# The feed-forward's second product: one 512-column matmul for both parts of the weights, and two VectorE sums for the halves

## The chip, the cores and the metric

The kernel runs on one core of a Trainium2 chip. The time is the device time of one execution in microseconds. The kernel before took 990.59 us (median of 3 runs, 989.98 to 991.91). The profiled execution took 988.45 us, of which its trace spans 986.7 us.

## The reference

It is one decoder block on 4 sequences of 1024 tokens with width 256: causal self-attention, cross-attention to 154 context tokens, both with 16 heads, and a feed-forward of width 1024, each added to the running `x`.

```python
nx = _ln(x, ln1_scale, ln1_bias);  qkv = nx @ W_qkv
x = x + _attend(q, k, v, causal) @ W_self_out
nx = _ln(x, ln2_scale, ln2_bias);  q, kv = nx @ W_q, encoder_output @ W_kv
x = x + _attend(q, k, v, None) @ W_cross_out
nx = _ln(x, ln3_scale, ln3_bias)
ffn = jax.nn.relu(nx @ W1 + b1) @ W2 + b2
return x + ffn
```

## The kernel before

One program of five instruction streams runs the stages in order: projections (A), self-attention, its output projection with the cross-attention's queries (C), cross-attention, and the last stage (E), which this change touches. Each engine works through its own stream in the order in which the code is written, and waits on semaphores. There is no scheduler.

Float32 products that need precision are made of three matmuls on rounded parts: each operand is split into a high part (its value rounded to the matmul's 32-bit format) and a low part (what is left). `product` (matmuls on lines 698, 699 and 700) adds high x low, low x high and high x high in the same accumulator. Every matmul loads its own stationary operand first.

Stage E treats 8 halves of a sequence (n = 0 to 7, 512 tokens each; `hf` is n's parity and picks its buffers). For one n:

- TensorE makes 8 feature blocks (`features_e`, f = 0 to 7, 512 tokens as columns, banks 0 and 1). Between them it makes the cross-attention's output projection for n + 1 (`project_e`).
- ScalarE applies bias and relu and rounds the result to `hT_hi`; VectorE makes `hT_lo` (line 1474). TensorE waits for each f by the semaphore `h_lo` in `part_in`.
- Then comes the second product, `relu(...) @ W2`, in four tiles t = 0 to 3 of 128 tokens and 256 output columns. The 8 feature blocks f are summed in a tile's accumulator. A bank holds 512 float32 columns, so tiles 0 and 1 fill bank 6 and tiles 2 and 3 fill bank 7. Once tile 1 is done TensorE transposes the normalised tokens of n + 1 (line 685, 8 transposes into banks 2 and 3), and goes on with tiles 2 and 3.
- ScalarE scales the transposed tokens of n + 1 (line 1023) and rounds them to `nT_hi` (line 1142); VectorE makes their low parts `nT_lo` (`scaled_low`, line 1429). Only behind this, in VectorE's stream, stand the two sums `xn = xt + bank` of n (line 1488, one for each bank, 512 columns), which free the banks by the semaphore `y_done`. `xt` holds the residual plus the bias `b2`.
- SyncE stores `xn` to the output after `y_done` (line 663).

`y_done` starts at 2, so that in n the tiles of bank 6 wait for the sum of bank 6 in n - 1, and the tiles of bank 7 for that of bank 7 in n - 1. The last n has no transposes and no `scaled_low`.

Of the kernel before, what the change touches and what calls it, by code (L numbers as in the profile page):

```python
# [5 lines left out]
ALU = mybir.AluOpType  # L6
# [4 lines left out]
F32R = mybir.dt.float32r  # L11

P = 128
# [5 lines left out]
def decoder_block_kernel(  # L19
# [3 lines left out]
    B, L, D = x.shape  # L23
# [4 lines left out]
    KC = D // P  # L28
    FC = F // P
    HF = 512  # L30
    TT = HF // P
# [32 lines left out]
    def tokens(ap, b, hf):  # L64
        return one(ap, b).rearrange("b (h t p) d -> p (b h) t d", p=P, t=TT)[:, hf]

    with ExitStack() as ctx:
        def sb(name, shape, dt=F32):
            return ctx.enter_context(nc.sbuf_tensor(name, shape, dt))

        def sem(name):
            return ctx.enter_context(nc.semaphore(name))

        bank = ctx.enter_context(nc.psum_tensor("bank", [P, 8, HF], F32))
# [31 lines left out]
        xt = sb("xt", [P, 2, TT, D])  # L106
# [6 lines left out]
        xn = sb("xn", [P, 2, TT, D])  # L113
# [38 lines left out]
        hT_hi, hT_lo = sb("hT_hi", [P, FC, HF], F32R), sb("hT_lo", [P, FC, HF], F32R)  # L152
        cT_hi, cT_lo = sb("cT_hi", [P, 2, KC, HF], F32R), sb("cT_lo", [P, 2, KC, HF], F32R)
        w1_hi, w1_lo = sb("w1_hi", [P, KC, F], F32R), sb("w1_lo", [P, KC, F], F32R)
        nT_hi, nT_lo = sb("nT_hi", [P, 2, KC, HF], F32R), sb("nT_lo", [P, 2, KC, HF], F32R)
        nxT_hi, nxT_lo = sb("nxT_hi", [P, 2, KC, HF], F32R), sb("nxT_lo", [P, 2, KC, HF], F32R)
        w2_hi, w2_lo = (t[:, :, :, :].rearrange("p h k (f d) -> p (h k f) d", d=D) for t in (nxT_hi, nxT_lo))
        wco_hi, wco_lo = sb("wco_hi", [P, KC, D], F32R), sb("wco_lo", [P, KC, D], F32R)
        HRING = 4
        hT = sb("hT", [P, HRING, HF])  # L160
# [46 lines left out]
        w_high, w_low = sem("w_high"), sem("w_low")  # L207
        wco_high, wco_low = sem("wco_high"), sem("wco_low")
        xb_ready = sem("xb_ready")
        f_ready, y_done = sem("f_ready"), sem("y_done")  # L210
        y_stored = [sem(f"y_stored{i}") for i in range(2)]

        class Attention:
# [168 lines left out]
        def _(sp):  # L382
            def load_x(ph, src, b, hf):
                sp.dma_start(xt[:, hf], tokens(src, b, hf)).then_inc(ph.x_in[hf], 16)
# [243 lines left out]
            def load_c(b, hf):  # L628
                if b == B - 1:
                    for half in range(2):  # L630
                        sp.wait_ge(XA.oC_stored[half], 16 + 16 * 2 * B)
                sp.dma_start(cT[:, hf], cross_ctx[bass.ds(2 * b, 2)].rearrange("c p t -> p c t")[:, :, HF * hf:HF * hf + HF]
                             ).then_inc(c_in[hf], 16)
# [20 lines left out]
            def store_e(b, left):  # L654
                for hf in range(2):
                    n = 2 * b + hf
                    if left > hf:
                        sp.wait_ge(E.xn_done, 2 + 2 * n + 4)
                        load_c(b + 1 + hf, 1 - hf)

                    for t0, t1 in ((0, TT),) if left or not hf else ((0, 2), (2, TT)):
                        sp.wait_ge(y_done, 2 + 2 * n + t1 // 2)
                        sp.dma_start(tokens(out, b, hf)[:, t0:t1],
                                     xn[:, hf, t0:t1]).then_inc(y_stored[hf], 16)
                    if left:
                        load_x(E, x1_dram, b + 1, hf)
# [3 lines left out]
            for b in range(B - 2):  # L670
                store_e(b, 2)
# [7 lines left out]
        def _(pe):  # L679
            def transposes(ph, n, hf, b0):  # L680

                pe.wait_ge(ph.nx_ready, n + 1)
                for k in range(KC):
                    for t in range(TT):
                        last = pe.transpose(bank[:, b0 + k, P * t:P * t + P], nx[:, hf, t, P * k:P * k + P], ident[:, :])  # L685
                    last.then_inc(ph.tp_ready, 1)
# [6 lines left out]
            def product(dst, terms, between=None):  # L693

                for j, (a_hi, a_lo, b_hi, b_lo) in enumerate(terms):
                    if between and j:
                        between(j - 1)
                    pe.matmul(dst, a_hi, b_lo, start=(j == 0), stop=False)  # L698
                    pe.matmul(dst, a_lo, b_hi, start=False, stop=False)  # L699
                    last = pe.matmul(dst, a_hi, b_hi, start=False, stop=(j == len(terms) - 1))  # L700
                return last
# [239 lines left out]
            def project_e(b, hf, i, o_bank=4):  # L941

                n = 2 * b + hf
                pe.wait_ge(c_lo, KC * n + KC)
                pe.wait_ge(E.xn_done, 2 + 2 * n + i - 1)
                for t in range(2 * i, 2 * i + 2):
                    last = product(bank[:, o_bank + i, D * (t % 2):D * (t % 2) + D],
                                   [(cT_hi[:, hf, k, P * t:P * t + P], cT_lo[:, hf, k, P * t:P * t + P], wco_hi[:, k, :],
                                     wco_lo[:, k, :]) for k in range(KC)])
                last.then_inc(E.o_ready, 1)  # L950
# [17 lines left out]
            def features_e(n, hf, f):  # L968
                pe.wait_ge(h_evac, 2 + FC * n + f - 1)
                product(bank[:, 1 - f % 2], [(w1_hi[:, k, P * f:P * f + P], w1_lo[:, k, P * f:P * f + P],  # L970
                                              nT_hi[:, hf, k, :], nT_lo[:, hf, k, :]) for k in range(KC)]
                        ).then_inc(h_ready, 1)
# [4 lines left out]
            def dense_e(b, more):  # L977
                for hf in range(2):
                    n = 2 * b + hf
                    ahead = hf == 0 or more  # L980
                    pe.wait_ge(nxT_low, 2 * n + 2)
                    for f in range(FC):
                        if n or f:
                            features_e(n, hf, f)
                        if f in PROJECT_AT and ahead:
                            pe.wait_ge(XA.acc_free, 2 + 2 * 4 * B)
                            project_e(b + hf, 1 - hf, PROJECT_AT.index(f))
                    pe.wait_ge(w_low, 3)


                    def part_in(f):
                        pe.wait_ge(h_lo, HRING + FC * n + f + 1)

                    for i in range(2):
                        pe.wait_ge(y_done, 2 + 2 * n + i - 1)
                        for t in range(2 * i, 2 * i + 2):
                            if t == 0:
                                part_in(0)
                            last = product(bank[:, 6 + i, D * (t % 2):D * (t % 2) + D],
                                           [(hT_hi[:, f, P * t:P * t + P], hT_lo[:, f, P * t:P * t + P], w2_hi[:, f, :], w2_lo[:, f, :])  # L1000
                                            for f in range(FC)], (lambda f: part_in(f + 1)) if t == 0 else None)
                        last.then_inc(f_ready, 1)
                        if i == 0 and ahead:
                            transposes(E, n + 1, 1 - hf, 2)

            pe.wait_ge(XA.exp_done, XA.SB + 4 * 4 * B * XA.NS)
# [161 lines left out]
        def _(dve):  # L1168
# [263 lines left out]
            def sums_e(b, hf, i, o_bank=4):  # L1432
                dve.wait_ge(y_stored[hf], 16 * b + 16)
                residual(E, b, hf, i, o_bank, 16)
# [33 lines left out]
            def dense_e(b, more):  # L1468
                for hf in range(2):
                    n = 2 * b + hf  # L1470
                    ahead = hf == 0 or more
                    for f in range(FC):
                        dve.wait_ge(h_hi, FC * n + f + 1)
                        dve.tensor_tensor(hT_lo[:, f, :], hT[:, f % HRING, :], hT_hi[:, f, :].bitcast(F32), ALU.subtract).then_inc(h_lo, 1)  # L1474
                        if f > PROJECT_AT[0] and f - PROJECT_AT[0] <= 2 and ahead:
                            sums_e(b + hf, 1 - hf, f - PROJECT_AT[0] - 1)
                        if f == PROJECT_AT[0] + 3 and ahead:
                            moments(E, xn, n + 1, 1 - hf)
                    if ahead:
                        normalize(E, xn, n + 1, 1 - hf)  # L1480
                    for k in range(KC) if more else ():
                        context_low(n + 2, hf, k)
                    if ahead:
                        scaled_low(n + 1, 1 - hf)
                    dve.wait_ge(xb_ready, n + 1)
                    for i in range(2):
                        dve.wait_ge(f_ready, 2 * n + i + 1)
                        dve.tensor_tensor(xn[:, hf, 2 * i:2 * i + 2, :], xt[:, hf, 2 * i:2 * i + 2, :],
                                          bank[:, 6 + i, :].rearrange("p (t d) -> p t d", t=2), ALU.add).then_inc(y_done, 1)

            dve.wait_ge(w_high, 2)
            dve.tensor_tensor(w2_lo, w2_sb[:, :, :], w2_hi.bitcast(F32), ALU.subtract).then_inc(w_low, 1)
# [219 lines left out]
```

## Time and profile before

| | |
|---|---|
| Median of 3 runs | 990.59 us |
| Profiled execution, and its span | 988.45 us, 986.7 us |
| TensorE busy with matmuls | 958.7 us (97%), 7632 matmuls |
| TensorE loading stationary operands | 599.0 us (61%) |
| VectorE busy | 742.7 us (75%) |
| ScalarE busy | 639.8 us (65%) |
| GpSimd busy | 257.2 us (26%) |
| Share of TensorE in the chain that ended last | 89% |

Busy time is a sum of the single instructions' durations where they don't overlap. A matmul's duration includes its way through the array, so two matmuls that follow each other overlap in the trace; what a matmul costs in a full stream is the distance between two starts, called its pitch here. "PEld" is the load of a stationary operand, which may run beside the matmul before it. A row of the timeline gives start, duration, engine, line, operation and count, and in brackets the idle time before it with what ended it.

### The profile page before, as it was taken

How to read it: one execution, taken by the hardware profiler on the slowest of the kernel's cores; microseconds unless marked ns; L12 is line 12 of the kernel's file. 1: busy time of each engine (PE TensorE's matmuls, PEld its weight loads, DVE VectorE, ACT ScalarE, POOL GpSimd, SP SyncE). 2: the span in 40 equal slices, each digit the busy share in tenths (PEclk: the TensorE clock that was granted, in tenths of full speed). 3: DMA queues.
4: the chain of work that ended last, by engine and by line, in shares of the span. 5: the costliest groups of instructions: out<-in, count | busy, mean ns of one | idle time of the engine just before them, and what ended most of it. 6: DMA issues, size and time to landing. Idle time of an engine off the chain costs nothing.

```text
span 986.7 us, 20078 instructions
## 1 busy us (share of the span) xinstructions
PE 958.7 (97%) x7632; PEld 599.0 (61%) x7632; DVE 742.7 (75%) x1175; ACT 639.8 (65%) x1371; POOL 257.2 (26%) x451
## 2 busy tenths in 40 slices
PE   4999999999999999999999999999999999999998
PEld 3876665445545555445443764444444699999997
DVE  7579779999999999999923787888887844455542
ACT  4653357777778787777777324888888644444543
POOL 6522123333222223232244210111114312222210
PEclk9999999999999999999999998999999999999999
DMA  6996762232323131313525887334441111122001
GB/s 210 316 352 230 247 195 90 80 99 68 110 67 109 56 100 59 102 52 104 173 90 169 270 318 234 99 124 145 139 130 36 64 55 54 65 65 64 23 21 43
DMA packets 78272, 124.01 MB, mean 126 GB/s; under 512 B 10624, under 2 KB 51872, under 8 KB 73120
## 3 DMA queue, kind: packets, MB, share of 16 engines
q1 hardware_dynamic: 78176, 122.73, 38.1%
q8 instruction: 60, 0.98, 0.4%
q14 instruction: 36, 0.29, 0.1%
HBM read 72.48 MB, written 49.17 MB: 123 GB/s over the span
## 4 chain that ended last, share of the span: by engine, by line
PE 89%; DVE 7%; ACT 1%; DMA 1%; SPq 1%; issue 1%; POOL 0%; ACTq 0%; DVEq 0%
PE bank L862 20%; PE bank L841 17%; PE bank L717 12%; PE bank L698 10%; PE bank L699 9%; PE bank L700 9%; DVE mx L1222 6%; PE bank L896 3%; PE bank L690 3%; PE bank L725 2%; PE bank L685 2%; DMA xt<-in_x_dram 1%; PE bank L738 1%; ACT probs L1115 1%; DVE probs L1215 1%
## 5 line engine op out<-in xcount | busy, mean ns | idle before, releaser
L1115 ACT ACTIVATE probs<-bank 128x512 f32<-128x512 f32 (+3 forms) x1024 | 456.8, 520 | 113.7 <-PE bank L841 107.1
L1222 DVE TENSOR_REDUCE mx<-bank 128x2 f32<-128x1024 f32 (+5 forms) x416 | 435.6, 1084 | 32.8 <-PE bank L717 19.9
L841 PE MATMUL bank<-q_st,k_st 64*128 64x512 f32 (+3 forms) x1024 | 265.9, 425 | 4.8 <-ACT probs L1115 3.5
L862 PE MATMUL bank<-probs,nx_mem 128*32 128x512 f32 (+3 forms) x2048 | 230.8, 528 | 0.4 <-POOL probs L1583 0.4
L841 PEld LDWEIGHTS bank<-q_st,k_st 64*128 64x128 f32 x1024 | 131.4, 186 | 154.4 <-ACT probs L1115 138.8
L717 PE MATMUL bank<-k_st,q_st 62*128 62x154 f32 (+4 forms) x1280 | 217.8, 352 | 4.8 <-DVE mx L1222 2.1
L717 PEld LDWEIGHTS bank<-k_st,q_st 62*128 62x128 f32 x1280 | 131.0, 188 | 71.9 <-DVE mx L1222 54.9
L1583 POOL TENSOR_SCALAR_AFFINE_SELECT probs<-probs 128x256 f32<-128x256 f32 x256 | 103.7, 409 | 198.4 <-ACT probs L1115 196.2
L1592 POOL TENSOR_TENSOR oN<-oT,rs 128x256 f32<-128x256 f32 x64 | 40.6, 635 | 212.8 <-DVE rs L1326 212.8
L1153 ACT ACTIVATE hT<-bank,b_sb 128x512 f32<-128x512 f32 x64 | 44.2, 690 | 72.7 <-PE bank L700 72.7
L1474 DVE TENSOR_TENSOR hT_lo<-hT,hT_hi 128x512 fp32r<-128x512 f32 x64 | 42.7, 687 | 54.5 <-ACT hT_hi L1156 53.5
L1030 ACT CAST probs<-bank 128x512 fp32r<-128x512 f32 x48 | 28.2, 587 | 77.9 <-PE bank L690 41.8
L1321 DVE STREAM_TRANSPOSE oT<-bank 128x512 f32<-128x512 f32 x64 | 45.7, 715 | 43.0 <-PE bank L862 42.8
L862 PEld LDWEIGHTS bank<-probs,nx_mem 128*32 128x32 f32 x2048 | 42.1, 108 | 57.6 <-issue 40.2
L698 PE MATMUL bank<-nxT_lo,hT_hi 128*128 128x256 f32 x256 | 75.3, 294 | 0.0
L699 PE MATMUL bank<-nxT_hi,hT_lo 128*128 128x256 f32 x256 | 72.4, 283 | 0.0
L700 PE MATMUL bank<-nxT_hi,hT_hi 128*128 128x256 f32 x256 | 72.3, 283 | 0.0
L725 PE MATMUL bank<-below,eye 64*128 64x64 bf16 (+1 forms) x1024 | 71.7, 208 | 0.0
L1524 POOL TENSOR_TENSOR veps<-mv,eps_sb 128x4 f32<-128x4 f32 x24 | 7.6, 317 | 199.8 <-DVE mv L1202 199.8
L1023 ACT ACTIVATE nxT<-bank,lnb_sb,lns_sb 128x512 f32<-128x512 f32 x44 | 31.9, 778 | 35.5 <-PE bank L685 35.5
L1215 DVE TENSOR_TENSOR probs<-bank,probs 128x512 fp32r<-128x512 f32 x48 | 32.9, 686 | 25.5 <-ACT probs L1030 25.4
L698 PEld LDWEIGHTS bank<-nxT_lo,hT_hi 128*128 128x128 f32 x256 | 48.9, 191 | 4.1 <-DVE hT_lo L1474 2.8
(126 smaller groups left out, 1263.7 us busy)
## 6 DMA issues: line engine op xcount, KB each, us to landing
q_st<-q_parts SPq DMA_DIRECT2D x48, 256.0 KB
q_st<-qx_parts SPq DMA_DIRECT2D x48, 256.0 KB
xt<-in_x_dram SPq DMA_DIRECT2D x16, 512.0 KB, 5.9
q_parts<-probs SPq DMA_DIRECT2D x16, 512.0 KB, 4.4
k_parts<-probs SPq DMA_DIRECT2D x16, 512.0 KB, 3.9
k_st<-k_parts SPq DMA_DIRECT2D x32, 256.0 KB
qx_parts<-probs SPq DMA_DIRECT2D x16, 512.0 KB, 4.8
v_aug<-vst_mem SPq DMA_DIRECT2D x8, 544.0 KB, 4.4
```

The lines of the kernel that those rows point to most:

```text
L698: pe.matmul(dst, a_hi, b_lo, start=(j == 0), stop=False)
L699: pe.matmul(dst, a_lo, b_hi, start=False, stop=False)
L700: last = pe.matmul(dst, a_hi, b_hi, start=False, stop=(j == len(terms) - 1))
L717: last = pe.matmul(banks[:, j, keys * y:keys * y + keys], q_st[w][h0:h0 + KROWS, i, P * qb:P * qb + P], keys_of(a, v0)[h0:h0 + KROWS, i, k ...
L725: last = pe.matmul(banks[:, j, end - width:end], eye[h0:h0 + HALF, e0:e0 + P], below[h0:h0 + HALF, 0:width], start=False, stop=width == HALF)
L841: pe.matmul(bank[:, score_bank(a, use), 0:n], keys_of(a, v0)[rows, i // 2, P * kb:P * kb + P], q_st[w][rows, i // 2, lo:lo + n], start=Tru ...
L862: last = pe.matmul(bank[32 * i:32 * i + 32, acc_bank(a, v0, hf), lo - HF * hf:lo - HF * hf + n], v_cur[w // 2][:, col:col + 32], probs[:, ...
L1115: act.activation(probs[:, use % NPT, 0:n], bank[:, score_bank(a, use), 0:n], ACT.Exp, scale=SCALE).then_inc(a.exp_done, 1)
L1153: act.activation(hT[:, f % HRING, :], bank[:, 1 - f % 2, :], ACT.Relu, bias=b1_sb[:, f:f + 1]).then_inc(h_evac, 1)
L1222: dve.tensor_reduce(mx[:, par, part].rearrange("p (j y) -> p j y", j=2)[:, :, blocks.start:blocks[-1] + 1:blocks.step], banks[:, :, 0:len( ...
L1321: dve.transpose(oT[:, hf].rearrange("p c d -> p (c d)"), bank[:, acc_bank(a, v0, hf), :]).then_inc(a.acc_free, 1)
L1583: pool.affine_select(out=tri, in_=tri, compare_op=ALU.is_ge, fill=0.0, base=0, pattern=[[0, 2], [1, P]], channel_multiplier=-1).then_inc(a ...
```

## The change

Per tile t and feature block f, `hT_hi x w2_lo` and `hT_hi x w2_hi` were two matmuls of 256 columns with the same stationary operand, each with its own load. They become one matmul of 512 columns: `w2_hi` and `w2_lo` now lie in one tensor `w2_parts`, and the matmul streams both. Its result is 512 columns wide, so that a tile now fills a bank: columns 0 to 255 hold the high weights' sum and 256 to 511 the low weights'. `hT_lo x w2_hi` stays a matmul of 256 columns and adds to the first half. The term of `hT_lo` for block f is now issued one block later, ahead of the matmul on `hT_hi` of block f + 1; in the last block both remaining ones come before it.

The tiles alternate between the banks 6 and 7, each tile waits for `y_done` of the tile two before it, and VectorE makes two sums of 256 columns for each tile, the second one waiting for the first by a new semaphore `y_half`.

```diff
-        nxT_hi, nxT_lo = sb("nxT_hi", [P, 2, KC, HF], F32R), sb("nxT_lo", [P, 2, KC, HF], F32R)
-        w2_hi, w2_lo = (t[:, :, :, :].rearrange("p h k (f d) -> p (h k f) d", d=D) for t in (nxT_hi, nxT_lo))
+        nxT_parts = sb("nxT_parts", [P, 2, 2 * KC * HF], F32R)
+        nxT_hi, nxT_lo = (nxT_parts[:, s].rearrange("p (h k t) -> p h k t", h=2, k=KC) for s in range(2))
+
+        w2_parts = nxT_parts[:, :, :].rearrange("p s (f d) -> p s f d", d=D)
+        w2_hi, w2_lo = w2_parts[:, 0], w2_parts[:, 1]
...
-                        sp.wait_ge(y_done, 2 + 2 * n + t1 // 2)
+                        sp.wait_ge(y_done, 2 + TT * n + t1)
...
-                    for i in range(2):
-                        pe.wait_ge(y_done, 2 + 2 * n + i - 1)
-                        for t in range(2 * i, 2 * i + 2):
+                    for t in range(TT):
+                        pe.wait_ge(y_done, TT * n + t + 1)
+                        for f in range(FC):
                             if t == 0:
-                                part_in(0)
-                            last = product(bank[:, 6 + i, D * (t % 2):D * (t % 2) + D],
-                                           [(hT_hi[:, f, P * t:P * t + P], hT_lo[:, f, P * t:P * t + P], w2_hi[:, f, :], w2_lo[:, f, :])
-                                            for f in range(FC)], (lambda f: part_in(f + 1)) if t == 0 else None)
+                                part_in(f)
+                            if f:
+                                pe.matmul(bank[:, 6 + t % 2, 0:D], hT_lo[:, f - 1, P * t:P * t + P], w2_hi[:, f - 1, :],
+                                          start=False, stop=False)
+                            if f == FC - 1:
+                                pe.matmul(bank[:, 6 + t % 2, 0:D], hT_lo[:, f, P * t:P * t + P], w2_hi[:, f, :], start=False, stop=False)
+                            last = pe.matmul(bank[:, 6 + t % 2, :], hT_hi[:, f, P * t:P * t + P], w2_parts[:, :, f, :],
+                                             start=(f == 0), stop=(f == FC - 1))
                         last.then_inc(f_ready, 1)
-                        if i == 0 and ahead:
+                        if t == 1 and ahead:
                             transposes(E, n + 1, 1 - hf, 2)
...
                     if ahead:
                         scaled_low(n + 1, 1 - hf)
                     dve.wait_ge(xb_ready, n + 1)
-                    for i in range(2):
-                        dve.wait_ge(f_ready, 2 * n + i + 1)
-                        dve.tensor_tensor(xn[:, hf, 2 * i:2 * i + 2, :], xt[:, hf, 2 * i:2 * i + 2, :],
-                                          bank[:, 6 + i, :].rearrange("p (t d) -> p t d", t=2), ALU.add).then_inc(y_done, 1)
+                    for t in range(TT):
+                        dve.wait_ge(f_ready, TT * n + t + 1)
+                        dve.tensor_tensor(xn[:, hf, t, :], xt[:, hf, t, :], bank[:, 6 + t % 2, 0:D], ALU.add).then_inc(y_half, 1)
+                        dve.wait_ge(y_half, TT * n + t + 1)
+                        dve.tensor_tensor(xn[:, hf, t, :], xn[:, hf, t, :], bank[:, 6 + t % 2, D:2 * D], ALU.add).then_inc(y_done, 1)
```

Below is TensorE's stream in n = 0 around the transposes for n + 1, before. The names are the program's, so the weights of the second product stand under the tensor whose place they take (`nxT_hi`, `nxT_lo`), and the transposed tokens under `nx_mem`.

```order
L698 MATMUL bank<-nxT_lo,hT_hi 128x256
L699 MATMUL bank<-nxT_hi,hT_lo 128x256
L700 MATMUL bank<-nxT_hi,hT_hi 128x256
L685 MATMUL bank<-ident,nx_mem 128x128 [waits E_nx_ready]
L685 MATMUL bank<-ident,nx_mem 128x128 x7
L698 MATMUL bank<-nxT_lo,hT_hi 128x256 [waits y_done]
L699 MATMUL bank<-nxT_hi,hT_lo 128x256
L700 MATMUL bank<-nxT_hi,hT_hi 128x256
```

The same place in the changed kernel, whose lines stand some numbers further down:

```order
L1005 MATMUL bank<-nxT_parts,hT_lo 128x256
L1008 MATMUL bank<-nxT_parts,hT_lo 128x256
L1009 MATMUL bank<-nxT_parts,hT_hi 128x512
L688 MATMUL bank<-ident,nx_mem 128x128 [waits E_nx_ready]
L688 MATMUL bank<-ident,nx_mem 128x128 x7
L1009 MATMUL bank<-nxT_parts,hT_hi 128x512 [waits y_done]
L1005 MATMUL bank<-nxT_parts,hT_lo 128x256
L1009 MATMUL bank<-nxT_parts,hT_hi 128x512
```

The transposes have kept their place behind tile 1. Behind them tile 2 waited for `y_done` of bank 7 in n - 1, and now waits for `y_done` of tile 0 in the same n.

VectorE's stream in n = 0 from the low parts of n + 1's tokens, before:

```order
L1424 TENSOR_TENSOR cT_lo<-vst_mem,cT_hi 128x512 [waits c_hi] x2
L1429 TENSOR_TENSOR nT_lo<-nxT,nT_hi 128x512 [waits nxT_high] x2
L1488 TENSOR_TENSOR xn<-xt,bank 128x512 [waits f_ready,xb_ready]
L1488 TENSOR_TENSOR xn<-xt,bank 128x512 [waits f_ready]
L1474 TENSOR_TENSOR hT_lo<-hT,hT_hi 128x512 [waits h_hi] x3
```

And in the changed kernel:

```order
L1433 TENSOR_TENSOR cT_lo<-vst_mem,cT_hi 128x512 [waits c_hi] x2
L1438 TENSOR_TENSOR nT_lo<-nxT,nT_hi 128x512 [waits nxT_high] x2
L1497 TENSOR_TENSOR xn<-xt,bank 128x256 [waits f_ready,xb_ready]
L1499 TENSOR_TENSOR xn<-xn,bank 128x256 [waits y_half]
L1497 TENSOR_TENSOR xn<-xt,bank 128x256 [waits f_ready]
L1499 TENSOR_TENSOR xn<-xn,bank 128x256 [waits y_half]
```

The sums still stand behind `nT_lo` of n + 1. Two of 512 columns have become eight of 256 columns (the first four are shown).

## Rows read from the trace of the kernel before

**Rows 1.** The page: busy us (share of the span) and instructions of each engine
```profile
PE 958.7 (97%) x7632; PEld 599.0 (61%) x7632; DVE 742.7 (75%) x1175; ACT 639.8 (65%) x1371; POOL 257.2 (26%) x451
```

**Rows 2.** The page: the chain that ended last, by engine
```profile
PE 89%; DVE 7%; ACT 1%; DMA 1%; SPq 1%; issue 1%; POOL 0%; ACTq 0%; DVEq 0%
```

**Rows 3.** The page's groups: the second product's high x high matmuls
```profile
L700 PE MATMUL bank<-nxT_hi,hT_hi 128*128 128x256 f32 x256 | 72.3, 283 | 0.0
```

**Rows 4.** Timeline, matmuls of 256 columns, three starts apart: start, us
```profile
791.07 0.28 PE L700 MATMUL bank<-nxT_hi,hT_hi 128*128 128x256 f32 x1
...
791.43 0.28 PE L700 MATMUL bank<-nxT_hi,hT_hi 128*128 128x256 f32 x1
```

**Rows 5.** Timeline, matmuls of 512 columns, three starts apart
```profile
783.94 0.39 PE L700 MATMUL bank<-nT_hi,w_hi 128*128 128x512 f32 x1
...
784.62 0.39 PE L700 MATMUL bank<-nT_hi,w_hi 128*128 128x512 f32 x1
```

**Rows 6.** Timeline, tile 0 of n = 0, with its waits for hT_lo
```profile
786.21 0.28 PE L698 MATMUL bank<-nxT_lo,hT_hi 128*128 128x256 f32 x1
...
788.69 0.19 PEld L698 LDWEIGHTS bank<-nxT_lo,hT_hi 128*128 128x128 f32 x1 [0.19 <-DVE hT_lo L1474]
...
789.29 0.19 PEld L698 LDWEIGHTS bank<-nxT_lo,hT_hi 128*128 128x128 f32 x1 [0.19 <-DVE hT_lo L1474]
...
789.63 0.28 PE L700 MATMUL bank<-nxT_hi,hT_hi 128*128 128x256 f32 x1
```

**Rows 7.** Timeline, TensorE from tile 1's end to tile 2's start, n = 0
```profile
792.51 0.28 PE L700 MATMUL bank<-nxT_hi,hT_hi 128*128 128x256 f32 x1
...
792.63 1.04 PE L685 MATMUL bank<-ident,nx_mem 128*128 128x128 f32 x8
...
793.42 0.36 PE L698 MATMUL bank<-nxT_lo,hT_hi 128*128 128x256 f32 x1
```

**Rows 8.** Timeline, ScalarE in the same stretch
```profile
793.27 1.45 ACT L1023 ACTIVATE nxT<-bank,lnb_sb,lns_sb 128x512 f32<-128x512 f32 x2 [4.11 <-PE bank L685]
794.61 1.14 ACT L1142 CAST nT_hi<-nxT 128x512 fp32r<-128x512 f32 x2
```

**Rows 9.** Timeline, VectorE in the same stretch
```profile
795.26 1.29 DVE L1429 TENSOR_TENSOR nT_lo<-nxT,nT_hi 128x512 fp32r<-128x512 f32 x2 [3.12 <-ACT nT_hi L1142]
796.47 0.68 DVE L1488 TENSOR_TENSOR xn<-xt,bank 128x512 f32<-128x512 f32 x1
799.46 0.69 DVE L1488 TENSOR_TENSOR xn<-xt,bank 128x512 f32<-128x512 f32 x1 [2.31 <-PE bank L700]
```

**Rows 10.** VectorE's groups by shape: line, op, shapes, count, busy us, mean ns
```profile
L1192 DVE BATCH_NORM_STATS2 stats<-xn 128x6 f32<-128x256 f32 x64 | 22.4, 413 | 0.3
...
L1215 DVE TENSOR_TENSOR partsx<-bank,partsx 128x154 fp32r<-128x154 f32 x8 | 2.5, 319 | 2.9 <-ACT partsx L1030 2.9
```

**Rows 11.** Timeline, two VectorE instructions with a wait of one for the other
```profile
640.52 0.28 DVE L1236 TENSOR_SCALAR nm<-bank 32x128 fp32r<-32x128 f32 x1
640.84 0.28 DVE L1238 SCALAR_TENSOR_TENSOR nm<-bank,nm 32x128 fp32r<-32x128 f32 x1
```

**Rows 12.** Timeline, VectorE's hT_lo whose end frees TensorE at 788.69
```profile
787.37 1.26 DVE L1474 TENSOR_TENSOR hT_lo<-hT,hT_hi 128x512 fp32r<-128x512 f32 x2
```

**Rows 13.** Timeline, the last of seven repeats, VectorE
```profile
956.46 1.29 DVE L1429 TENSOR_TENSOR nT_lo<-nxT,nT_hi 128x512 fp32r<-128x512 f32 x2 [4.32 <-ACT nT_hi L1142]
```

**Rows 14.** Timeline, VectorE's last sum, ahead of the last store
```profile
983.43 0.69 DVE L1488 TENSOR_TENSOR xn<-xt,bank 128x512 f32<-128x512 f32 x1 [5.00 <-PE bank L700]
```

**Rows 15.** Timeline, the kernel's first matmuls of 512 columns, after an idle stretch
```profile
15.02 0.79 PE L698 MATMUL bank<-nxT_lo,wqk_hi 128*128 128x512 f32 x1 [2.52 <-DVE nxT_lo L1254]
...
16.46 0.63 PE L698 MATMUL bank<-nxT_lo,wqk_hi 128*128 128x512 f32 x1
...
17.32 0.63 PE L700 MATMUL bank<-nxT_hi,wqk_hi 128*128 128x512 f32 x1
```

**Rows 16.** Windows there: stretch, us, PE busy (x), PEclk, DMA share, GB/s
```profile
15.00:20.00 5.00, 3.49 (x11) 1.00 0.42 149
```

More of the change, by code:

```diff
@@ L209, in decoder_block_kernel @@
         xb_ready = sem("xb_ready")
-        f_ready, y_done = sem("f_ready"), sem("y_done")
+        f_ready, y_half, y_done = sem("f_ready"), sem("y_half"), sem("y_done")
         y_stored = [sem(f"y_stored{i}") for i in range(2)]
```

## The prediction

> **What bounds the kernel now.** I read the page first: TensorE is busy for 97% of the span [rows 1] and makes up 89% of the chain that ended last [rows 2]. Whatever TensorE is kept waiting for is therefore added to the time, and whatever it is spared is taken off, unless a wait swallows it. Then I read the timeline of stage E, where the 256 triples of the second product stand (8 halves x 4 tiles x 8 blocks) [rows 3]. In a full stream a triple of 256-column matmuls takes 0.36 us, start to start [rows 4], so 0.120 us each; three of 512 columns take 0.68 us, 0.227 us each [rows 5]. TensorE has one place in n where it waits, in tile 0: twice for `hT_lo` [rows 6]. Between tile 1 and tile 2 it does not wait: eight transposes follow the last product within 0.12 us, and tile 2 starts at 793.42 [rows 7]. VectorE at that moment is idle until 795.26, because ScalarE must first scale and round what TensorE has just transposed [rows 8], then makes `nT_lo`, and only at 796.47 begins the sum of tiles 0 and 1 [rows 9]. Before, nobody needed that sum soon. The same picture comes 7 times, at n = 0 to 6, from 795.26 to 956.46 [rows 9, 13], so every (956.46 - 795.26) / 6 = 26.87 us.
>
> **The matmuls.** A triple becomes a matmul of 256 columns and one of 512: 0.120 + 0.227 = 0.347 us instead of 0.36, 0.0133 us less. The columns are the same 768; what goes is the fixed part that each matmul has beside its columns (256 more columns cost 0.227 - 0.120 = 0.107 us, so about 0.013 us of the 0.120 is fixed). In tiles 1 to 3 that is 24 triples x 0.0133 = 0.32 us for each n, 2.56 us for 8. The trace has no matmul of 512 columns read in two separate pieces. Bounds: without any fixed part 768 columns would take 3 x 0.107 = 0.32 us, 0.04 us less, 7.7 us over 192 triples; if the wide matmul costs two of 256, nothing is saved. I take 0.0133, since the loads, 0.19 us each and three in 0.36 us, already overlap the matmuls.
>
> The Trainium skill, in "TensorE: Matmul & The Clock Gate", section "Back-to-back issue gap", gives an isolated matmul at full clock its columns at 2.4 GHz plus 2.5 ns. By that a triple would save 2.5 ns and the 192 would save 0.5 us, not 2.56. The trace disagrees in size: both pitches here lie above that formula, and I go by the rows.
>
> Tile 0 gains nothing. Its last wait for `hT_lo` ends at 789.29 and tile 1 starts at 789.63 + 0.12 = 789.75, 0.46 us later [rows 6]. That moment is set by ScalarE and VectorE and stays. Behind it now stand low (block 6), low (block 7) and the wide one: 0.12 + 0.12 + 0.227 = 0.467, plus the 0.10 that a first matmul after a wait costs extra (0.46 - 0.36), so 0.57 us. That is 0.11 us more, 0.85 us for 8 halves.
>
> **The wait that is added.** Bank 6 now holds only tile 0, so tile 2 needs `y_done` of tile 0 in the same n. VectorE gives it behind `nT_lo` of n + 1, which needs ScalarE's rounding, which needs the transposes that TensorE issues right ahead of tile 2. So TensorE waits for a round trip that starts with its own work. Its length:
> - VectorE can begin the sums at 796.47, as it did before [rows 9].
> - A sum of 256 columns is not in the trace. Nearest rows: 0.413 us for 256 columns of another VectorE operation, 0.319 us for a tensor_tensor with 154 columns from a bank [rows 10], and 0.68 us for 512 columns of the same sum [rows 9]. I take 0.42 us, with 0.32 and 0.68 as ends.
> - The second sum waits for the first. Such a pair left 640.84 - 640.52 - 0.28 = 0.04 us between [rows 11].
> - VectorE's release reaches TensorE in 788.69 - (787.37 + 1.26) = 0.06 us [rows 6, 12].
>
> TensorE resumes at 796.47 + 0.42 + 0.04 + 0.42 + 0.06 = 797.41, instead of 793.42: 3.99 us, in 7 of 8 halves, 27.9 us. Nothing hides it: TensorE's stream is in order and behind tile 2 stand tile 3 and the next half's 8 feature blocks, which are the kernel's bound. Their operand `nT_lo` is ready in both versions. With the ends for the sum the term is 26.5 to 31.6 us.
>
> The other new waits are met. Tile 3 needs tile 1's sums, 0.9 us behind tile 0's, while tile 2 takes 8 x 0.347 = 2.8 us. Tile 0 of n + 1 needs tile 2's, long done. Tile 1 of n + 1 needs tile 3's, which end 0.9 us behind the product. In n = 7 no transposes stand between, VectorE has nothing ahead of the sums, and tile 1's 2.8 us cover tile 0's. VectorE's next work, `hT_lo` of block 0, waits for TensorE and ScalarE anyway. At the end of the kernel the last store waits for 0.42 + 0.04 + 0.42 = 0.88 us of sums instead of 0.69 [rows 14]: 0.19 us. The bigger `y_done` counts for SyncE cost nothing, and the new layout of `w2_parts` moves no instruction.
>
> **The sum.** 27.9 + 0.85 + 0.19 - 2.56 = +26.4 us. On the profiled execution's 988.45 us that is 1014.8; that execution lies 2.1 us under the median of 990.59, so I predict 990.59 + 26.4 = 1017 us. With all ends of the unknown terms set against it: -5.1 and -1.4 down, +2.6 and +3.7 up, 1010.5 to 1023. That is the forecast's own range.
>
> **Rivals.**
> *The clock falls in the new gap.* Before, TensorE never stops in stage E for as long as 4 us. After its idle stretches at the start of the kernel its first matmuls of 512 columns stood (17.32 - 16.46) / 2 = 0.43 us apart, which is 512 columns at 1.2 GHz, the lower of the two levels, instead of 0.227 [rows 15, 5]; the granted clock reads 1.00 there all the same [rows 16], so it would not show it. Six such matmuls lost 6 x 0.2 = 1.2 us. Once per gap that is 8.4 us; if all of tiles 2 and 3 ran at half speed, 5.6 us per gap, 39 us. I take 1.4 us per gap, near the row: 10 us, 1027 us (1025 to 1056). For it: the gap is new, and repeats 7 times. Against it: no row shows how a gap of 4 us between full streams ends. A quarter.
> The Trainium skill holds, on the same page in "Why this matters for your kernels", that idle gaps between bursts of matmuls send the clock back to half; by that rule the time is this rival's, and no stretch of the trace tests it with such a gap.
>
> *The wide matmul costs two.* The change does not do what it says: w2's two parts lie 8 KB apart in a partition, and if the read breaks there, nothing is saved. Then 26.4 + 2.56 = 29 us, 1019.6 us. Against it: 512-column matmuls read at the full rate everywhere. 8%.
>
> *The gap closes, not slower.* Tiles 0 and 1 are done while VectorE idles 3.12 us ahead of `nT_lo` [rows 9]; if the sums ran there, tile 2 would find its bank free, and the 27.9 us would go: 0.85 + 0.19 - 2.56 = -1.5 us, 989.1 us. It decides if the wait is under 0.2 us per half. Against it: VectorE's stream has the sums behind `nT_lo`, and engines have nowhere in this trace taken such instructions out of order. 2%.
>
> **How the numbers follow.** Forecast 63%, clock 25%, no saving 8%, closed gap 2%, others 2%. The time is the forecast's, 1017 us. The range, 1013 to 1029, leaves out the forecast's low end, the far part of the clock's case and the closed gap, about 2 in 10. A measurement of this kernel tells about 0.2% (2 us) from no change. Faster by more than that 2%, within it 2%, slower 96%.
>
> **What would show it.** In the profile after: 7 idle times of TensorE of about 4.0 us between the transposes and tile 2, released by VectorE's second sum, 28 us in all, where now there is none. The n-to-n distance grows from 26.87 to about 30.7 us. A pair of 256 and 512 columns takes 0.347 us; 0.36 would mean no saving, 0.32 no fixed part. A sum takes 0.42 us. If the matmuls behind the gap stand at 0.24 and 0.43 us, the clock has fallen. The forecast is wrong if TensorE's idle time in stage E stays under some 20 us, or the time is under 1010 us.

## The result, and the profile after

The changed kernel takes 1029.61 us (median of 4 runs, 1029.0 to 1030.22), 1.039 times the kernel before (95% interval 1.0369 to 1.0411), 39.0 us more. The profiled execution took 1030.22 us.

The page after: TensorE is busy for longer in absolute terms, and for less of the span (95%, before 97% [rows 1]). In the chain that ended last TensorE's share has fallen from 89% to 82%, VectorE's has risen from 7% to 12% and ScalarE's from 1% to 3% [rows 2].

```profile
span 1028.5 us, 19614 instructions
PE 973.9 (95%) x7376; PEld 596.3 (58%) x7376; DVE 757.8 (74%) x1223; ACT 639.7 (62%) x1371; POOL 256.6 (25%) x451
PEclk9999999999999999999999989999999898999989
...
PE 82%; DVE 12%; ACT 3%; issue 1%; DMA 0%; SPq 0%; POOL 0%; DVEq 0%; ACTq 0%
```

The third line is the granted clock in 40 slices: it dips in the last quarter of the span, where stage E stands. The dip further ahead, where the cross-attention begins, stands in the page before too. TensorE's waits (line, releaser: us in total, times, longest) have a new first entry, 7 times 3.7 us:

```profile
PE bank L1009 <- DVE xn L1499: 26.0, 7, 3.7
PE bank L688 <- DVE nx_mem L1217: 12.0, 2, 10.5
```

TensorE's timeline in n = 0, which answers to [rows 7] and goes on into tile 2:

```profile
793.97 1.03 PE L688 MATMUL bank<-ident,nx_mem 128*128 128x128 f32 x8
798.73 0.80 PE L1009 MATMUL bank<-nxT_parts,hT_hi 128*128 128x512 f32 x1 [3.72 <-DVE xn L1499]
799.32 0.42 PE L1005 MATMUL bank<-nxT_parts,hT_lo 128*128 128x256 f32 x1
799.53 0.63 PE L1009 MATMUL bank<-nxT_parts,hT_hi 128*128 128x512 f32 x1
799.97 0.41 PE L1005 MATMUL bank<-nxT_parts,hT_lo 128*128 128x256 f32 x1
...
804.66 0.44 PE L1009 MATMUL bank<-nxT_parts,hT_hi 128*128 128x512 f32 x1
804.94 0.28 PE L1005 MATMUL bank<-nxT_parts,hT_lo 128*128 128x256 f32 x1
805.06 0.40 PE L1009 MATMUL bank<-nxT_parts,hT_hi 128*128 128x512 f32 x1
```

Before, the first matmul of tile 2 stood 0.79 us behind the transposes' start, now 4.76 us: 3.97 us more. And it runs slowly: from 799.32 to 799.97 a pair takes 0.65 us. That is 768 columns at 1.2 GHz, the lower level; only from 804.94 on do pairs take 0.35 us again. The windows (stretch, us, time that TensorE was busy with its number of instructions, granted clock, DMA share, GB/s) give the granted clock:

```profile
798.73:804.66 5.93, 5.93 (x19) 0.50 0.00 0
```

VectorE in the same half, answering to [rows 9]. The first two sums of 256 columns free tile 2's bank; the 4.80 and 2.25 us are its waits for the slow tiles 2 and 3:

```profile
796.60 1.29 DVE L1438 TENSOR_TENSOR nT_lo<-nxT,nT_hi 128x512 fp32r<-128x512 f32 x2 [3.17 <-ACT nT_hi L1151]
797.80 0.42 DVE L1497 TENSOR_TENSOR xn<-xt,bank 128x256 f32<-128x256 f32 x1
798.25 0.42 DVE L1499 TENSOR_TENSOR xn<-xn,bank 128x256 f32<-128x256 f32 x1
...
804.26 0.42 DVE L1497 TENSOR_TENSOR xn<-xt,bank 128x256 f32<-128x256 f32 x1 [4.80 <-PE bank L1009]
804.71 0.42 DVE L1499 TENSOR_TENSOR xn<-xn,bank 128x256 f32<-128x256 f32 x1
807.39 0.42 DVE L1497 TENSOR_TENSOR xn<-xt,bank 128x256 f32<-128x256 f32 x1 [2.25 <-PE bank L1009]
```

**Where the time went.** From the transposes of n = 0 to the end the span was 986.7 - 792.63 = 194.1 us before and is 1028.5 - 793.97 = 234.5 us, 40.5 us more; the other 1.3 us of the spans' difference stood ahead of 27 us already, where the change does nothing: the eight transposes at 19.44 took 1.94 us in this execution and 1.06 before, and the matmuls stayed at half rate for a while behind them. The 40.5 us are:
- 7 waits of 3.97 us: 27.8 us.
- 7 stretches of tiles 2 and 3 at the lower clock. From tile 2's start to tile 3's first sum they take 8.66, 7.38, 8.21, 7.20, 7.42, 7.43 and 8.25 us, and 5.95 us where the clock stays up (third experiment): 12.9 us, 1.84 us for each.
- The rest nearly cancels out: tiles 1 to 3 take up to 2.82 instead of 2.88 us, tile 0 takes 0.11 us more, and the end 0.2 us more.

### The profile page after: what moved, and what is told of

The parts are those of the page before. It is cut to its first block, busy times and chain, and to the rows that moved or that the text cites. A ratio compares the mean times of both kernels' runs of the same rounds, so it can differ in the third digit from the quotient of the medians.

```text
span 1028.5 us, 19614 instructions
## 1 busy us (share of the span) xinstructions
PE 973.9 (95%) x7376; PEld 596.3 (58%) x7376; DVE 757.8 (74%) x1223; ACT 639.7 (62%) x1371; POOL 256.6 (25%) x451
## 4 chain that ended last, share of the span: by engine, by line
PE 82%; DVE 12%; ACT 3%; issue 1%; DMA 0%; SPq 0%; POOL 0%; DVEq 0%; ACTq 0%
PE bank L865 19%; PE bank L844 16%; PE bank L720 12%; PE bank L1009 6%; DVE mx L1231 6%; PE bank L701 5%; PE bank L703 5%; PE bank L702 5%; PE bank L1005 3%; PE bank L899 3%; PE bank L693 3%; PE bank L728 2%; DVE hT_lo L1483 2%; PE bank L688 2%; ACT hT_hi L1165 1%
## 5 line engine op out<-in xcount | busy, mean ns | idle before, releaser
L1009 PE MATMUL bank<-nxT_parts,hT_hi 128*128 128x512 f32 x256 | 103.5, 441 | 26.0 <-DVE xn L1499 26.0
L1009 PEld LDWEIGHTS bank<-nxT_parts,hT_hi 128*128 128x128 f32 x256 | 53.5, 214 | 37.8 <-DVE xn L1499 27.7
L1005 PE MATMUL bank<-nxT_parts,hT_lo 128*128 128x256 f32 x224 | 70.5, 315 | 0.6
L1005 PEld LDWEIGHTS bank<-nxT_parts,hT_lo 128*128 128x128 f32 x224 | 48.1, 215 | 8.9 <-DVE hT_lo L1483 7.7
```

What stands on the lines that cost most here:

```text
L1005: pe.matmul(bank[:, 6 + t % 2, 0:D], hT_lo[:, f - 1, P * t:P * t + P], w2_hi[:, f - 1, :], start=False, stop=False)
L1009: last = pe.matmul(bank[:, 6 + t % 2, :], hT_hi[:, f, P * t:P * t + P], w2_parts[:, :, f, :], start=(f == 0), stop=(f == FC - 1))
```

## The experiments

Two theories stood against each other. The first says that the wait and the lower clock both come from the banks and VectorE's order; the second, that the wide matmuls themselves cost more or bring the clock down.

**e1_sums_first: the order alone, undone.** VectorE makes the sums of tiles 0 and 1 ahead of `nT_lo`; `sums_y` holds what the loop over the tiles held.

```diff
+                    dve.wait_ge(xb_ready, n + 1)
+                    sums_y((0, 1))
                     if ahead:
                         scaled_low(n + 1, 1 - hf)
-                    dve.wait_ge(xb_ready, n + 1)
-                    for t in range(TT):
...
+                    sums_y((2, 3))
```

> The changed kernel, with VectorE's sums of tiles 0 and 1 ahead of the low parts of the next half's tokens. Theory (the time went into a wait that VectorE's order makes, and into a lower clock that this wait brings on): no wait between the transposes and tile 2, granted clock 1.00 in the last stage, 7 x 3.97 = 27.8 us and some 14 us of slow matmuls gone. What is left of the change is 3 x 8 tiles at 2.82 instead of 2.88 us (-1.5), tile 0 (+0.9) and the end (+0.2): 990.2 us. Rival (the wide matmuls themselves bring the clock down or cost more than two narrow ones): clock still under 1.00 in the last stage, 1000 us or more.

Measured: 991.79 us, 1.000 (0.9983 to 1.0018) times the kernel before. The wait is gone and the clock reads 1.00 over the whole last stage:

```profile
797.14:990.40 193.26, 189.25 (x1017) 1.00 0.16 50
```

The 193.3 us from the transposes to the end are 0.8 us less than before (194.1). So the wide matmuls bring no slow clock, and alone they are worth about nothing. VectorE's timeline shows that the early sums cost nothing either: they stand where VectorE would have idled, and `nT_lo` still waits for ScalarE. It starts 2.62 us behind the transposes (797.14), before 2.63.

```profile
796.95 0.42 DVE L1497 TENSOR_TENSOR xn<-xn,bank 128x256 f32<-128x256 f32 x1
...
797.79 0.42 DVE L1497 TENSOR_TENSOR xn<-xn,bank 128x256 f32<-128x256 f32 x1
...
799.76 1.29 DVE L1438 TENSOR_TENSOR nT_lo<-nxT,nT_hi 128x512 fp32r<-128x512 f32 x2 [1.55 <-ACT nT_hi L1151]
```

**e2_narrow_split: the banks and waits without the wide matmul.**

```diff
-                            last = pe.matmul(bank[:, 6 + t % 2, :], hT_hi[:, f, P * t:P * t + P], w2_parts[:, :, f, :], ...)
+                        last = product(bank[:, 6 + t % 2, 0:D], [(hT_hi[...], hT_lo[...], w2_hi[:, f, :], w2_lo[:, f, :]) ...], ...)
...
-                        dve.tensor_tensor(xn[:, hf, t, :], xn[:, hf, t, :], bank[:, 6 + t % 2, D:2 * D], ALU.add).then_inc(y_done, 1)
```

> The changed kernel's banks, waits and order, with the old matmuls: each tile has three matmuls of 256 columns a block in its own bank, and one VectorE sum of 256 columns. Theory (wait and clock come from the banks and the order, not from the wide matmul): TensorE waits 7 times 3.97 - 0.46 = 3.5 us, 24.6 us in all, and the clock falls after it as in the changed kernel, some 10 to 14 us: 1025 to 1029 us. Rival (the wide matmul brings the clock down): waits of 3.5 us, clock at 1.00, 990.6 + 24.6 = 1015 us.

Measured: 1027.8 us, 1.037 (1.0338 to 1.0408). The waits are 7 x 3.3 us of idle time (tile 2 starts 4.30 us behind the transposes' start, 3.51 more than before, as expected). The clock falls as much; three of the seven windows behind the waits, the other four read 0.50 to 0.72:

```profile
PE bank L701 <- DVE xn L1492: 22.9, 7, 3.3
```

```profile
828.00:834.00 6.00, 5.83 (x28) 0.53 0.00 0
861.00:867.00 6.00, 6.00 (x37) 0.72 0.01 3
892.88:898.00 5.12, 5.12 (x24) 0.50 0.00 0
```

From tile 2's start to tile 3's sum it is 7.44 to 8.58 us, where before it was 6.04 (799.46 - 793.42 [rows 7, 9]): 13.4 us in all, as much as in the changed kernel (12.9). The loss belongs to the banks and the order. The width of the matmul has a part in it only by the second sum that it needs, 0.46 us of each wait.

**e3_fill16: the wait without the idleness.**

```diff
                         if t == 1 and ahead:
                             transposes(E, n + 1, 1 - hf, 2)
+                            for _ in range(16):
+                                pe.matmul(bank[:, 0, :], hT_hi[:, 0, 0:P], w2_parts[:, :, 0, :], start=True, stop=True)
```

> The changed kernel with 16 matmuls of 512 columns into bank 0, which is free then, ahead of tile 2's wait: their result is used by nothing. Theory (the clock falls because TensorE is idle): the 16 take 16 x 0.227 = 3.6 us of the 3.97 us of the wait and cost nothing, the clock stays at 1.00, tiles 2 and 3 take 5.6 us, and the time is 1029.6 - 13.7 = 1016 us. Rival (the clock falls for another reason, as the width of the matmuls): 1029 us as before.

Measured: 1016.98 us, 1.027 (1.0239 to 1.03). TensorE is busy with work that nobody needs, and the necessary work behind it runs at full clock. The median is 12.6 us lower than the changed kernel's; the two were measured at different times, but from the transposes of n = 0 to the end the profiles say the same: 1018.6 - 797.13 = 221.5 us instead of 234.5. Here are tile 2's start and tile 3's first sum, 5.95 us apart, and the window of the whole stage:

```profile
797.92 3.92 PE L1015 MATMUL bank<-nxT_parts,hT_hi 128*128 128x512 f32 x16
801.88 0.50 PE L1009 MATMUL bank<-nxT_parts,hT_hi 128*128 128x512 f32 x1
```

```profile
807.83 0.42 DVE L1499 TENSOR_TENSOR xn<-xt,bank 128x256 f32<-128x256 f32 x1 [1.94 <-PE bank L1009]
```

```profile
797.00:1018.60 221.60, 217.13 (x1130) 1.00 0.14 43
```

This splits the 39 us: 13 us are the clock, and 26 us are the wait, less the little that the wide matmuls save. In this stage the clock falls because TensorE is idle.

**e4_before_sums_first: the control for the order of the sums.** In the kernel before, the sum of bank 6 goes ahead of `scaled_low`.

> The kernel before, with VectorE's sum of bank 6 ahead of the low parts of the next half's tokens: the control for the order of the sums. Theory: VectorE is idle for 3.1 us there, so the low parts are not later, and the time is that of before, 990.6 us within 1 us. Rival (the early sum delays the low parts and with them the next half): several us slower.

Measured: 990.76 us, 0.9993 (0.9972 to 1.0014); one of the ten executions took 2837.14 us, for which nothing on record gives a cause. The old kernel did not care where its sums stood, which is why nobody had to think about it.

**e5_fill8 and e11_fill4: the idle time's length.** As e3, with `range(8)` and `range(4)`.

> The changed kernel with only 8 matmuls of 512 columns (1.8 us) in the gap, so that TensorE then idles for about 2.1 us ahead of tile 2. If a shorter idle time still brings the clock down as often and as long, tiles 2 and 3 take as long as in the changed kernel (7.6 us on average) and the time is 1029 us. If it is the length of the idle time that counts, they take 5.6 us and the time is 1016 us as with 16 matmuls. Theory: the second, or between the two.

> The changed kernel with 4 matmuls of 512 columns in the gap, so that TensorE then idles for about 2.8 us ahead of tile 2. With 0, 8 and 16 the idle times were 3.7, 1.9 and none, and the clock fell after 7, 1 and 0 of 7 gaps. If the length of the idle time decides, the clock falls after some or all of the 7 gaps, and each costs 1 to 3 us: 1018 to 1030 us. If only the full gap does it: 1017 us.

Measured: 1021.77 us, 1.030 (1.0272 to 1.0328), and 1022.5 us, 1.0306 (1.0275 to 1.0337). In each profile, counted by the seven times from tile 2's start to tile 3's first sum (5.95 us at full clock):

| idle ahead of tile 2 | clock fell | extra us of each fall |
|---|---|---|
| 3.7 us (changed kernel) | 7 of 7 | 1.2 to 2.7 |
| 3.3 us (e2, against 6.04 us) | 7 of 7 | 1.4 to 2.5 |
| 2.8 us (e11) | 2 of 7 | 2.7, 1.5 |
| 1.9 us (e5) | 1 of 7 | 1.5 |
| none (e3) | 0 of 7 | |

The window behind e5's first gap shows its one fall, and then come the first two gaps of e11, where the restart is slow from the first matmul on (0.80 us), and a later one, where it isn't (0.50 us):

```profile
802.02:806.00 3.98, 3.98 (x14) 0.59 0.00 0
```

```profile
801.17 0.80 PE L1009 MATMUL bank<-nxT_parts,hT_hi 128*128 128x512 f32 x1 [2.80 <-DVE xn L1501]
834.68 0.80 PE L1009 MATMUL bank<-nxT_parts,hT_hi 128*128 128x512 f32 x1 [2.80 <-DVE xn L1501]
```

```profile
897.76 0.49 PE L1009 MATMUL bank<-nxT_parts,hT_hi 128*128 128x512 f32 x1 [2.79 <-DVE xn L1501]
```

In these kernels a longer idle time brings more falls, and even 1.9 us can bring one. The counts are from one profile each.

The medians of e5 and e11 lie 5 us above e3, more than one or two falls explain. In the profiles stage E takes what the falls say: from the transposes of n = 0 to the end 222.8 us in e5 and 225.7 in e11, 1.4 and 4.2 more than e3's 221.5, where the falls cost 1.5 and 4.2. The rest lies in other executions, or ahead of stage E: that stage starts up to 5.2 us apart between profiles whose earlier stages are the same (transposes of n = 0 at 792.09 in e2, 792.63 before, 797.26 in e5). A part of this may be the clock too: from 30 to 785 us the windows add up to 10.2 us at the lower level before, in the changed kernel and in e2, and to 13.6 or 13.7 in e1, e3, e5 and e11. What makes one execution differ from the next stays open.

**e6_hi_first, e8_before_hi_first and e7_both_wide_first: what stands behind the last wait.** What stands behind tile 0's last wait for `hT_lo` decides its length. In e6, on top of e1, tile 0's wide matmuls go first and the eight on `hT_lo` last; e8 does the same in the kernel before, with narrow matmuls; e7 takes the wide ones of tiles 0 and 1 ahead of all on `hT_lo`, which needs a bank for each tile:

```diff
+                    pe.wait_ge(y_done, TT * n + 2)
+                    for f in range(FC):
+                        pe.wait_ge(h_hi, FC * n + f + 1)
+                        for t in range(2):
+                            wide(t, f)
                     for t in range(TT):
...
+                            if t < 2:
+                                last = narrow(t, f, f == FC - 1)
```

> Sums ahead of the low parts as in the first experiment, and in tile 0 all 8 wide matmuls before the 8 on hT_lo. Theory (tile 0 waits for hT_lo, whose last block comes at a fixed time, and what stands behind that wait is what tile 0 costs): behind the last wait stands one matmul of 256 columns, 0.22 us instead of 0.57, so tile 0 takes 3.3 instead of 3.65 us, 8 x 0.35 = 2.8 us less than the first experiment's kernel: 987 to 988 us. Rival (tile 0 is bound by its matmuls): no change, 990.6 us.

> The kernel before, with its narrow matmuls and shared banks, and in tile 0 the 16 matmuls on hT_hi ahead of the 8 on hT_lo. Behind the last wait for hT_lo stands one matmul instead of three, 0.22 instead of 0.46 us: 8 x 0.24 = 1.9 us less, 988.7 us. It shows how much of the sixth and seventh kernels' gain needs no wide matmul. Rival: no change.

> As the sixth, with the wide matmuls of tiles 0 and 1 alternating ahead of all matmuls on hT_lo of both; each has its own bank, which the change made possible. Theory: the wait for hT_lo is covered whole, tiles 0 and 1 together take 2 x 2.82 = 5.6 us instead of 3.65 + 2.82 = 6.47, 8 x 0.83 = 6.6 us less than the first experiment's kernel: 984 us. Rival (a wait comes back elsewhere, as the transposes' normalised tokens that are now wanted 0.8 us earlier, or tile 0's sums ahead of tile 2): 987 us or more, with TensorE waiting ahead of the transposes or tile 2.

Measured: e6 987.47 us, 0.9965 (0.9949 to 0.9981); e8 989.33 us, 0.9984 (0.9967 to 1.0); e7 985.38 us, 0.9946 (0.9923 to 0.9969). The first came as expected; e8 lies where it was expected, at the edge of what can be told from no change. The intervals of e6 and e8 overlap, but their traces tell them apart: from one half's transposes to the next's it is 26.40 us in e6 where e1 has 26.73, and 26.62 in e8 where the kernel before has 26.87. The order alone earns 0.33 us a half with wide matmuls and 0.25 with narrow ones. In e7 tiles 0 and 1 take 5.54 us, as they should, but a half takes (949.12 - 791.32) / 6 = 26.30 us where e1's takes 26.73, so some 3.4 of the 6.6 us arrived: tile 2 starts 1.22 us behind the transposes' start instead of 0.79, since tile 0's sums stand behind other VectorE work.

```profile
785.78 3.79 PE L1000 MATMUL bank<-nxT_parts,hT_hi 128*128 128x512 f32 x16
789.41 2.08 PE L1004 MATMUL bank<-nxT_parts,hT_lo 128*128 128x256 f32 x16
791.32 1.04 PE L688 MATMUL bank<-ident,nx_mem 128*128 128x128 f32 x8
792.54 0.50 PE L1000 MATMUL bank<-nxT_parts,hT_hi 128*128 128x512 f32 x1 [0.19 <-DVE xn L1512]
```

```profile
790.42 1.28 DVE L1448 TENSOR_TENSOR cT_lo<-vst_mem,cT_hi 128x512 fp32r<-128x512 f32 x2
791.62 0.41 DVE L1510 TENSOR_TENSOR xn<-xt,bank 128x256 f32<-128x256 f32 x1
```

**e9_sums_before_context: the best version.** On top of e7, the sums of tiles 0 and 1 go ahead of `cT_lo` as well.

```diff
                     dve.wait_ge(xb_ready, n + 1)
+                    sums_y((0, 1))
                     for k in range(KC) if more else ():
                         context_low(n + 2, hf, k)
-                    sums_y((0, 1))
```

> The seventh experiment's kernel, with VectorE's sums of tiles 0 and 1 ahead of the low parts of the attention context too, two instructions of 0.6 us each. In the seventh, tile 2 began 0.43 us late, as those two stood ahead of tile 0's sums. Theory: tile 0's sums end about 0.6 us before tile 2 wants the bank, no wait, a half every 25.9 instead of 26.3 us, 7 x 0.4 = 2.8 us less: about 982.5 us. Rival (the low parts of the context, now later, delay the next half's projection): no gain, and TensorE waits in the next half.

Measured: 982.77 us, 0.9912 (0.9893 to 0.9931), faster than both kernels. Tile 2 follows the transposes again after 0.80 us, and a half takes (925.90 - 796.79) / 5 = 25.8 us instead of 26.87.

```profile
794.06 1.04 PE L688 MATMUL bank<-ident,nx_mem 128*128 128x128 f32 x8
794.86 0.47 PE L1000 MATMUL bank<-nxT_parts,hT_hi 128*128 128x512 f32 x1
```

```profile
796.79 1.28 DVE L1453 TENSOR_TENSOR nT_lo<-nxT,nT_hi 128x512 fp32r<-128x512 f32 x2
...
925.90 1.28 DVE L1453 TENSOR_TENSOR nT_lo<-nxT,nT_hi 128x512 fp32r<-128x512 f32 x2
```

**e10_contiguous: is a read in two pieces dear?** e1 with `w2_parts` laid out so that a block's two parts lie side by side.

> The first experiment's kernel with the two parts of the weights side by side for each block, so that the wide matmul reads 512 columns in one piece. A pair of a narrow and a wide matmul takes 0.353 us in the changed kernel, not the 0.347 that was forecast. If the read in two pieces costs this, pairs fall to 0.347 and the time by 256 x 0.006 = 1.5 us against the first experiment's kernel. Theory: the pair stays at 0.353, since what costs is the change from narrow to wide matmul, and the time stays.

Measured: 990.21 us, 0.9989 (0.9973 to 1.0004), the same as e1. A half takes (928.78 - 795.00) / 5 = 26.76 us, in e1 (930.79 - 797.14) / 5 = 26.73. The layout makes no difference. My reason for a dearer pair is not borne out as put: in both kernels a tile's pairs take from 0.346 to about 0.355 us. In e1 for n = 0 (below) it is 0.345 in tile 2 (798.71 to 799.05 and to 799.40) and 0.355 in tile 1 (795.01 to 795.37 and to 795.72), but for n = 2 tile 2 has 0.356. Why the tiles differ was not tried.

```profile
795.01 0.40 PE L1009 MATMUL bank<-nxT_parts,hT_hi 128*128 128x512 f32 x1
...
795.37 0.40 PE L1009 MATMUL bank<-nxT_parts,hT_hi 128*128 128x512 f32 x1
...
795.72 0.40 PE L1009 MATMUL bank<-nxT_parts,hT_hi 128*128 128x512 f32 x1
...
798.71 0.39 PE L1009 MATMUL bank<-nxT_parts,hT_hi 128*128 128x512 f32 x1
...
799.05 0.40 PE L1009 MATMUL bank<-nxT_parts,hT_hi 128*128 128x512 f32 x1
...
799.40 0.39 PE L1009 MATMUL bank<-nxT_parts,hT_hi 128*128 128x512 f32 x1
```

## Why the prediction was wrong, point by point

The direction was right, and so was the wait. The size was not: 1017 us (26.4 more) was forecast with a range to 1029, and 1029.6 (39.0 more) came.

- **The matmuls.** Forecast 0.0133 us saved per triple, 2.56 us in all. Measured in e1: pairs of 0.346 to 0.356 us. A tile takes 2.79 or 2.82 us where 2.88 stood, 0.06 to 0.09 us of the 0.107 forecast; e1, which holds all of the change but the wait, gained nothing that can be told from no change.
- **Tile 0.** Forecast 0.11 us longer. It takes 791.15 - 787.50 = 3.65 us, against 789.75 - 786.21 = 3.54: as forecast. (The row at 790.92 below holds its last wide matmul and tile 1's first, which starts 0.23 us later.)

```profile
787.50 0.39 PE L1009 MATMUL bank<-nxT_parts,hT_hi 128*128 128x512 f32 x1
...
790.92 0.62 PE L1009 MATMUL bank<-nxT_parts,hT_hi 128*128 128x512 f32 x2
```

- **The wait.** Forecast 3.99 us, 7 times, released by VectorE's second sum. Measured 3.97 us, 7 times. Its parts fit too: a sum 0.42 us, 0.03 us between the two, 0.06 us to TensorE.
- **The other new waits** were met, as said: none shows in TensorE's waits.
- **The step that failed** is the choice between the forecast and the first rival. The sum 27.9 + 0.85 + 0.19 - 2.56 has no term for the clock: it kept TensorE's clock up across seven new gaps, and the fall, measured at 12.9 us, stood in it at nothing. I gave the fall a quarter, because no row showed how a gap between two full streams ends. In fact the clock fell after every one of the seven. e3 shows that this alone is 12.6 us: without it the time is 1016.98 us, the forecast's number. The same stands in the distance from one half's transposes to the next's: 30.7 us was forecast, and (989.33 - 793.97) / 6 = 32.56 came, 1.8 us more. The sign named for this rival came as well: behind the gap matmuls start 0.21 and 0.44 us apart (799.32, 799.53, 799.97). The rival's mechanism was right, its price too low: 1.4 us a gap taken from the opening's six slow matmuls, where 1.84 was measured. The row gave a lower bound of that cost, since the opening's slow stretch was cut short by TensorE's next idle time, and I took a value next to it. With 1.84 the rival comes to 990.6 + 26.4 + 12.9 = 1029.9 us.
- **A wrong detail.** I wrote that the granted clock would not show the fall, since it reads 1.00 in the opening [rows 16], where matmuls ran at half rate. In stage E it does show it, 0.50 from 798.73 to 804.66. And the trace of the kernel before has two falls that I overlooked, both in the attention stages. In windows of 1 us the granted clock is low from 530.3 to 533.7, where TensorE shows no idle time at all, and from about 608.8 to 615.6, where its longest idle time shortly ahead was 0.8 us. So it was on record before the change both that the granted clock shows a fall and what one can cost: where TensorE is busy throughout, half of such a stretch would be lost, 1.7 or 3.4 us (an estimate from these two lengths), where I took 1.4.

```profile
530.00:535.00 5.00, 5.00 (x29) 0.66 0.56 144
610.00:615.00 5.00, 4.93 (x28) 0.50 0.57 171
```

- **The range** ended at the near side of the rival that came true. It held that rival's lower price only.

The Trainium skill's rule that I weighed there ("TensorE: Matmul & The Clock Gate", section "Why this matters for your kernels": idle gaps between bursts send the clock to half) was the better guide here. The trace agrees, with 7 falls in 7 gaps of 3.7 us; e11 and e5 show falls behind shorter gaps too, 2.8 and 1.9 us.

## What to carry to other kernels

Where a change gives each tile a whole bank, ask who frees the bank and what stands ahead of that in its stream: here two sums that nobody had waited for became the end of a round trip that starts with TensorE's own transposes, and moving them a few lines up takes 38 us back. A wait of several microseconds on a TensorE that was never idle costs its length and then the slow matmuls behind it, here almost half as much again; put both into the sum. Before you give the clock a chance, look in the trace before for every stretch where it is low already. And look at what follows the last wait of a tile: putting there what needs the late operand, and nothing else, earned more (e6, e7, e9) than joining the matmuls did (e1).

## What the runs showed of the hardware

- In stage E, after an idle time of 3.3 to 3.7 us between full streams the clock fell in 14 of 14 cases; after 2.8 us in 2 of 7 and after 1.9 us in 1 of 7. Each fall cost 1.2 to 2.7 us of extra time on the matmuls behind it.
- A fall can come after the restart: in the gap before 929.53 the first matmul took 0.50 us, as at full clock (e3: 0.50), and the tile turned slow only from about 931.0 on.

```profile
929.53 0.50 PE L1009 MATMUL bank<-nxT_parts,hT_hi 128*128 128x512 f32 x1 [3.72 <-DVE xn L1499]
...
933.14 1.05 PE L1009 MATMUL bank<-nxT_parts,hT_hi 128*128 128x512 f32 x2
```

- The clock can also fall without such a gap: in the kernel before it did at 530.3 us, where TensorE was busy throughout with attention's matmuls of 64 rows or 32 output partitions, and at about 608.8, behind idle times of 0.8 us at most. No run varies this.
- Sixteen matmuls that nobody needs, put into a gap, make the kernel 12.6 us faster than leaving TensorE idle there.
- 512 moving columns that lie in two pieces 8 KB apart stream as fast as in one piece (a half takes 26.73 us in e1 and 26.76 in e10).
